# One instruction for the decay products, six bias rows folded away, scores in four 64x64 tiles, and new lists

## The reference, cut to what matters

```python
# one layer; l = 0 on ctx, l = 1 on x, l = 2 on both outputs
k = key @ kW.T + kb;  q = query @ kW.T + kb;  v = values @ vW.T + vb
sc = softmax(where(dam, q @ k.T / sqrt(32), NEG))      # first softmax
dist = sqrt((sum(sc) - cumsum(sc)) * |i - j|)
te = clip(exp(dist * -softplus(gammas)), 1e-5, 1e5)
att = softmax(where(mask & dam, scores * te, NEG)) @ v
x = layernorm(query + att @ oW.T + ob) * ln1_g + ln1_b
if l != 1:                                             # feed-forward
    x = layernorm(x + relu(x @ w1.T + b1) @ w2.T + b2) * ln2_g + ln2_b
# cross attention of x on ctx
scores = (x @ wq) heads (ctx @ wk).T / 4 * pad - (1 - pad) * 1e10
x = layernorm(softmax(scores) @ (ctx @ wv) @ wo + bo + x) * ln_gamma + ln_beta
```

## Time and profile before

| | value |
|---|---|
| median of 3 runs | 3373.02 us (3371.89 to 3376.1) |
| the profiled execution | 3372.7 us, its span 3371.0 us |
| PE busy | 2990.0 us, 89% |
| DVE busy | 2802.8 us, 83% |
| ACT busy | 2715.9 us, 81% |
| POOL busy | 775.8 us, 23% |
| mean granted TensorE clock | 0.97 |

### The profile page before, as it was taken

The page is one execution under the profiler, slowest core; times in us unless marked ns, Lnnn a source line. Parts: engine busy times, 40 slices in busy tenths (PEclk is TensorE's granted clock), DMA queues, the critical chain, the costliest instruction groups (busy, mean ns, idle before and its releaser), DMA issues.

```text
span 3371.0 us, 71476 instructions
## 1 busy us (share of the span) xinstructions
PE 2990.0 (89%) x19520; PEld 2204.6 (65%) x19520; DVE 2802.8 (83%) x5825; ACT 2715.9 (81%) x10244; POOL 775.8 (23%) x1111
## 2 busy tenths in 40 slices
PE   2689999999999999999999999999999998999986
PEld 1466676666676666676666666666666666666664
DVE  3688988888988888988888988888988888988883
ACT  1688888888888888888888888888888887888883
POOL 1212222222222222222222221222221222221221
PEclk9799999999999999999999999999999999999998
DMA  5000101000101000101100001000101101001100
GB/s 160 20 25 25 32 25 33 27 26 25 30 25 33 27 26 25 30 25 33 28 26 25 29 24 33 29 26 25 28 24 33 29 28 29 24 24 33 29 17 10
DMA packets 166407, 101.66 MB, mean 30 GB/s; under 512 B 36697, under 2 KB 165709, under 8 KB 166221
## 3 DMA queue, kind: packets, MB, share of 16 engines
q1 hardware_dynamic: 166220, 99.97, 10.4%
HBM read 56.26 MB, written 10.01 MB: 20 GB/s over the span
## 4 chain that ended last, share of the span: by engine, by line
PE 55%; DVE 19%; issue 12%; SPq 4%; ACT 3%; DMA 2%; POOL 1%; DVEq 0%; ACTq 0%; POOLq 0%
PE gen_ps L623 17%; PE gen_ps L755 13%; PE gen_ps L709 6%; PE gen_ps L673 4%; SPq L556 4%; PE gen_ps L690 3%; DVE E L920 3%; PE scores_ps L664 2%; ACT X L802 2%; PE scores_ps L652 2%; DVE X L929 2%; PE gen_ps L718 2%; PE gen_ps L631 2%; PE gen_ps L684 2%; DVE res L964 2%
## 5 line engine op out<-in xcount | busy, mean ns | idle before, releaser
L802 ACT ACTIVATE X<-X,nm 128x128 f32<-128x128 f32 x1536 | 596.0, 405 | 56.7 <-DVE nm L945 55.8
L802 ACT ACTIVATE E<-scores_ps,nm 128x128 f32<-128x128 f32 x1536 | 542.3, 406 | 24.2 <-DVE nm L912 24.0
L912 DVE TENSOR_REDUCE nm<-scores_ps 128x8 f32<-128x1024 f32 x320 | 390.3, 1220 | 182.0 <-PE scores_ps L652 113.6
L623 PE MATMUL gen_ps<-f_buf,up_w 128*128 128x256 f32 x2048 | 466.1, 383 | 0.8 <-ACT f_buf L459 0.8
L1052 POOL TENSOR_SCALAR_AFFINE_SELECT X<-X 128x1024 f32<-128x1024 f32 x192 | 211.2, 1100 | 1100.8 <-DVE X L939 1100.0
L755 PE MATMUL gen_ps<-down_w,hidden 128*128 128x256 f32 x2048 | 459.7, 379 | 0.0
L802 ACT ACTIVATE X<-scores_ps,nm 128x128 f32<-128x128 f32 x1024 | 362.3, 400 | 116.6 <-issue 60.9
L673 PE MATMUL gen_ps<-ident,X 128*128 128x128 f32 x2560 | 380.0, 283 | 79.2 <-ACT xv_t L476 39.8
L929 DVE SCALAR_TENSOR_TENSOR X<-E,rz,decay 128x128 f32<-128x128 f32 x1536 | 431.0, 350 | 3.7 <-DVE E L920 0.5
L920 DVE TENSOR_TENSOR_SCAN E<-chain,E 128x1024 f32<-128x1024 bf16 x192 | 429.8, 2238 | 0.0
L623 PEld LDWEIGHTS gen_ps<-f_buf,up_w 128*128 128x128 f32 x2048 | 382.7, 191 | 70.5 <-issue 21.9
(11 more groups left out here) (124 smaller groups left out, 5491.7 us busy)
## 6 DMA issues: line engine op xcount, KB each, us to landing
k_diag<-k_f SPq DMA_DIRECT2D x768, 32.0 KB, 1.9
xk_diag<-xk_f SPq DMA_DIRECT2D x1024, 8.0 KB, 1.8
ctx_f<-in_ctxT SPq DMA_DIRECT2D x32, 256.0 KB, 3.2
ctx_t<-in_ctx SPq DMA_DIRECT2D x32, 256.0 KB, 2.8
x_f<-in_xT SPq DMA_DIRECT2D x32, 256.0 KB, 2.6
x_t<-in_x SPq DMA_DIRECT2D x32, 256.0 KB, 2.6
cx_f<-in_ctxT SPq DMA_DIRECT2D x32, 256.0 KB, 2.7
out<-out_t SPq DMA_DIRECT2D x32, 256.0 KB, 2.2
```

The lines of the kernel that those rows point to most:

```text
L623: mm = nc.tensor.matmul(ps[:, i * T:(i + 1) * T], w[:, k, c * P:(c + 1) * P], src[:, k, :], start=(k == 0), stop=(k == C - 1))
L802: a = nc.scalar.activation(dst[:, cols], src[:, cols], ACT.Exp, bias=minus_max[:, h:h + 1], accum_out=sums[:, h:h + 1])
L912: nc.vector.tensor_reduce(nm1[:, UNIT[u], :], unit_heads(scores_ps[SLOT[u]][:, :]), AX_X, ALU.max, negate=True).then_inc(max1_done, 1)
```

## The change

It does five things.

1. `dist` loses its reciprocal, and `x` becomes one tensor_tensor of 1024 columns (scan times decay). The reciprocal of the sums moves behind the square root: a new POOL step `zroot` computes -(z1 ** -0.5) for eight columns in two instructions, and `effect` on ACT becomes eight activations of 128 columns whose scale is that column.
2. Of nine bias rows three stay (o of layers 0 and 1, v of layer 2). vb of layers 0 and 1 is folded into ob by matmuls with o_w, the other four (ob of layer 2, both b2, bo) are added to norm_b in the prologue, and what they would add behind a norm is taken out of up_bias, k_bias and a new q_bias. `q` on its reader becomes two instructions with a bias.
3. The mask (or padding) and the scores matmuls are each four 64x64 tiles. dam_bias has a new layout, filled by 24 DMAs rather than 3; pad_bias is loaded by two DMAs. The waits of `scores` stand apart from the matmuls.
4. The prologue gets 4 matmuls of 256 columns and 40 of one column on PE for the folds, with DVE work and three DMAs behind them, before the first projection. The three row_bias DMAs now wait for this.
5. All lists and BANKS are new. TENSOR and SYNC hold the same steps in another order. From SCALAR to VECTOR go up (0,2), (0,3), (2,1); k 0; q; turn (0,2), (2,1), (0,1); pt (3,1,0) both halves, (2,0) half 0, (0,1) both, (1,0) half 0. From VECTOR to SCALAR go v 1, v 2; up (2,0); pt (3,0,1) half 1, (3,0,0) both, (3,1,1) half 1. POOL gets six zroot steps.

```diff
 def distance(now, d, u):
-    for i in range(UH):
-        ins = nc.vector.scalar_tensor_tensor(out=X[:, p, i * S:(i + 1) * S],
-                                             in0=E[:, E_SLOT[u], i * S + 1:(i + 1) * S + 1],
-                                             scalar=rz1[:, UNIT[u], i:i + 1], in1=decay[:, l, i, :],
-                                             op0=ALU.mult, op1=ALU.mult)
-    ins.then_inc(x_done, 1)
+    nc.vector.tensor_tensor(X[:, X_SLOT[u], :], E[:, E_SLOT[u], 1:UW + 1],
+                            decay[:, u[0], :, :].rearrange("p h s -> p (h s)"), ALU.mult).then_inc(x_done, 1)
 def effect(now, d, u):
-    nc.scalar.activation(x, x, ACT.Exp, scale=-1.0).then_inc(te_done, 1)
+    act.wait_ge(zroot_done, zroot_order.upto(now, d, ("zroot", u)))
...
+    for i in range(UH):
+        cols = slice(i * S, (i + 1) * S)
+        a = nc.scalar.activation(x[:, cols], x[:, cols], ACT.Exp, scale=rz1[:, n, i:i + 1])
+    a.then_inc(te_done, 1)
+def zroot(now, d, u):
+    n = UNIT[u]
+    wait_apart(pool, exp1_done, exp1_order.upto(now, d, ("exp1", u)))
+    nc.gpsimd.tensor_tensor(rz1[:, n, :], z1[:, n, :], neg_half[:, :], ALU.pow).then_inc(zpow_done, 1)
+    wait_apart(pool, zpow_done, zroot_order.upto(now, d, ("zroot", u)))
+    nc.gpsimd.tensor_scalar(rz1[:, n, :], rz1[:, n, :], -1.0, None, ALU.mult).then_inc(zroot_done, 1)
 # scores
+for bank, half in quarters:                      # (0,0), (0,1), (1,0), (1,1)
+    rows = halves[bank]
+    dst = out[halves[half], bank * BANK:(bank + 1) * BANK]
+    if is_layer(u):
+        nc.tensor.matmul(dst, ident_bf[rows, rows], dam_bias[u[0]][rows, half, :], start=True, stop=False)
...
+for i in range(n):                               # n = 2 for a layer unit, 1 for a cross unit
+    for bank, half in quarters:
...
+        mm = nc.tensor.matmul(out[halves[half], bank * BANK + i * wide:bank * BANK + (i + 1) * wide],
+                              q[rows, i if is_layer(u) else u[2], queries], keys,
+                              start=False, stop=(i == n - 1))
 # prologue on PE
+for l in range(2):
+    for k in range(C):
+        mm = nc.tensor.matmul(rows_ps[0:ROWS, 0:D], v_cols[:, l, k, :], o_w[l][:, k, :], ...)
+def fold(col, w, which):
+    for k in range(C):
+        mm = nc.tensor.matmul(cols_ps[:, col:col + 1], w[:, k, :], bias_cols[:, which, k:k + 1], ...)
...                                              # 16 folds of up_w, 2 of k_w, 2 of xq_w
 # prologue on SP
-for l in range(L):
-    sp.dma_start(dam_bias[l][:, :, :], src).then_inc(toeplitz_in, 16)
+for l in range(L):
+    for bank in range(2):
+        for c in range(C):
+            for half in range(2):
+                sp.dma_start(dst.rearrange("p (j s) -> p j s", s=S), src).then_inc(toeplitz_in, 16)
...
+sp.wait_ge(rows_ready, 1)
+for i in range(3):
+    sp.dma_start(row_bias[i:i + 1, :, :], rows_parts[:, i, :]).then_inc(rows_out, 16)
```

Of the new orders the prediction speaks of these stretches:

```diff
 TENSOR
-(1, ("down", 2)), (0, ("att", (0, 1))), (0, ("att", (0, 0))), (1, ("turn", 2, 2))
+(1, ("down", 2)), (0, ("att", (0, 1))), (1, ("vx",)), (1, ("turn", 2, 2))
-(1, ("scores", (3, 0, 1))), (0, ("pt", (1, 1), 1)), (0, ("att", (1, 0))), (0, ("att", (1, 1))), (1, ("scores", (3, 0, 0)))
+(1, ("scores", (3, 0, 1))), (1, ("scores", (3, 0, 0)))
 VECTOR
-(1, ("sums", 2, 2)), (0, ("max2", (1, 0))), (0, ("scores2", (1, 1))), (1, ("tok", 2, 2))
+(1, ("sums", 2, 2)), (0, ("max2", (1, 0))), (1, ("tok", 2, 2))
 POOL
+(0, ("zroot", (1, 0))), (2, ("dev", 3, 1)), (0, ("zroot", (1, 1))), (0, ("widen", (0, 1))), (0, ("select", (1, 0)))
```

More of the change, by code:

```diff
@@ L34 @@
 FIRST_KEY_MASK = [1, 1, 0]
+BIAS_COLS = 6
+ROWS = 3
+O_ROWS, V2_ROW = (0, 1), 2
 FFN_LAYERS = [0, 2]
@@ new lines @@
+POOL = [(1, ("dev", 0, 2)), (1, ("widen", (2, 1))), (0, ("zroot", (0, 1))), (1, ("widen", (2, 0))),
+    (0, ("zroot", (0, 0))), (0, ("select", (0, 0))), (1, ("dev", 2, 1)), (0, ("select", (0, 1))),
+    (0, ("zroot", (1, 0))), (2, ("dev", 3, 1)), (0, ("zroot", (1, 1))), (0, ("widen", (0, 1))),
+    (0, ("select", (1, 0))), (0, ("widen", (0, 0))), (1, ("dev", 2, 2)), (0, ("select", (1, 1))),
+    (0, ("widen", (1, 0))), (0, ("widen", (1, 1))), (0, ("dev", 0, 1)), (0, ("dev", 1, 1)),
+    (1, ("widen", (3, 0, 1))), (1, ("widen", (3, 0, 0))), (1, ("widen", (3, 1, 0))), (0, ("zroot", (2, 1))),
+    (0, ("zroot", (2, 0))), (0, ("select", (2, 1))), (0, ("select", (2, 0))), (1, ("widen", (3, 1, 1)))]
@@ L191 @@
     kind_order(SCALAR, kind) for kind in ("ln", "root", "effect", "exp2", "spread"))
-select_order, dev_order, wide_order = (kind_order(POOL, kind) for kind in ("select", "dev", "widen"))
+select_order, dev_order, wide_order, zroot_order = (kind_order(POOL, kind) for kind in ("select", "dev", "widen", "zroot"))
 GEN_BANKS = 4
@@ L583, in load @@
                     wait_apart(sp, scores_done, scores_order.upto(now, d, last, 1))
-                    sp.dma_start(pad_bias[0:3, :], pad_parts_dram[:, tok]).then_inc(done, 16)
+                    for first in (0, HALF):
+                        sp.dma_start(pad_bias[first:first + 3, :], pad_parts_dram[:, tok]).then_inc(done, 16)
             def store(now, g, d):
@@ new lines, in scores @@
+                halves = [slice(i * HALF, (i + 1) * HALF) for i in range(2)]
+                quarters = ((0, 0), (0, 1), (1, 0), (1, 1))
+                wait_apart(pe, scores_free[p], bank_order[p].before(now, d, ("scores", u)))
+                if not is_layer(u):
+                    wait_apart(pe, loaded["pad_bias"], 32 * (g + 1))
+                for bank, half in quarters:
[3 more added lines that the diff above has]
+                        nc.tensor.matmul(dst, ident_bf[rows, rows], dam_bias[u[0]][rows, half, :], start=True, stop=False)
+                    else:
+                        bias = pad_bias[rows, b * S:(b + 1) * S].unsqueeze(1).to_broadcast([HALF, BANK // S, S])
+                        nc.tensor.matmul(dst, pad_ones[rows, :], bias, start=True, stop=False)
@@ L708, in out_proj @@
                     for c in range(C):
-                        nc.tensor.matmul(out, att[:, b, c, :], w[:, c, :], start=(c == 0), stop=False)
-                    mm = add_row(out, row)
+                        mm = nc.tensor.matmul(out, att[:, b, c, :], w[:, c, :], start=(c == 0), stop=(c == C - 1 and l > 1))
+                    if l < 2:
+                        mm = add_row(out, O_ROWS[l])
                 return mm
@@ L869, in _, with split @@
             link(nc.vector.tensor_scalar(pads[:, :], pads[:, :], -1.0, PAD_BIAS, ALU.add, ALU.mult))
-            for whole, parts in ((pads, pads_parts), (rows, rows_parts)):
+            def split(whole, parts, ready):
                 for i in range(3):
```

226 lines of the change are left out of this document (131 added, 95 removed), and 52 rows, old and new, of tables (SCALAR, TENSOR, VECTOR).

## The result

The changed kernel takes 3452.89 us (median of 4 runs, 3451.61 to 3454.56) against 3373.78 for the kernel before, measured beside it: 1.0234 times as long, interval 1.0217 to 1.0252. 3291 was predicted, with 3190 to 3395 as range: the time is slower and outside the range, 162 us above the forecast.

What follows compares the result with a forecast made beforehand. It took PE's work, 92.4 us of a 100.64 us turn, plus some 8 us of waiting as the bound. Prologue 86 + 31 turns of 97.2 + 190 ramp and run out + 1.7 gave 3291 us, range 3190 to 3395.

Steps and rivals of the forecast that it cites:

- Durations and work: Busy time a turn after the change: PE 88.2 us, ACT 88.5, DVE 85.3, built from traced instruction times.
- bound of 99 us a turn: Upper bound for the turn: PE waits 10.8 us, called midway to DVE's present 13.9.
- rival of weights that show between 64x64 tiles: PE's score tiles: 32 sets each show 0.10 us of weight loading, turn 100.5, total 3397 us; chance 0.06.
- What is taken from PE counts nearly whole, until ACT or DVE is as full: Work removed from PE, 92.4 to 88.2 us a turn, was to shorten the turn almost fully.
- A turn after ... 97.2: Turn after the change, down from 100.64 us, with waits of 9.0 on PE, 8.7 ACT, 11.9 DVE.
- from 7 to 21 us on 24.0, still the emptiest ... which hides it: POOL's six powers and negations add 7 to 21 us a turn, hidden by 5.3 us of other work.
- new orders answer for that: POOL's list: dev, widen and select wait behind the power's wait on exp1; reordering was to deal with it; no size.
- POOL late: POOL's widen and power meet scans, delaying select, dev and tok twice a turn by 1 us: 99.2, 3355 us; chance 0.07.
- ACT takes over: The effect on ACT, in every unit's chain, lengthens waits to 13 us: turn 101.5, total 3430 us; chance 0.13.
- Some 2 of the 3.4 us there should go: PE's longest gap, ahead of the transpose of x_tok, shrinks by some 2 us, perhaps with the slow clock stretch.
- what is late next I can't read: The next late step in the new lists was left unnamed; a slipped DVE tok could cost PE up to 5 us.
- The prologue: Before the first projection: mask DMAs, norm rows and folds add 26 to 37 us, taken as +29, to 86 us.

## Why the prediction was wrong

By its own steps:

- **Durations and work: right.** PE 89.2 against 88.2; the folds' rows 1.1 where 1.3 was forecast; the tiles 1.8 where 2.6 was forecast for the old lists (2.9 less the 0.3 of two cross units side by side), though each unit measures as worked out (0.24 and 0.96). ACT 88.1 against 88.5, effect 2.4 us as from the earlier trace rows; in the new lists part 1 adds 7.6 to ACT (88.0 less 80.4; 8.0 forecast, though the row it names gives 8.6) and takes 6.0 from DVE (6.5 forecast). The read-outs that move to DVE are 2.5 us (84.7 to 80.6 on ACT is the forecast 4.0, 87.0 to 89.5 on DVE is half of its 5.0). In the bound of 99 us a turn, midway from 8.2 to 13.9 is 11.1 and not 10.8; nothing hangs on it. The rival of weights that show between 64x64 tiles is refuted by 0.96 us from the scores to the next group, where four sets that showed 0.10 each would have given 1.36. The rule that the prediction quotes beside it from the Trainium skill (TensorE: Matmul & The Clock Gate) stands there in the section "The mechanism"; the trace disagrees with it, as the prediction says.
- **"What is taken from PE counts nearly whole, until ACT or DVE is as full": this step failed.** Taken from PE in the old lists, 3.5 us brought 1.0, 1.8 brought none, 1.1 brought 0.5. Folds and tiles alone have 99.9 a turn where the prediction's terms gave 96.7: 3.2 of the 5.2 us by which the turn was missed. The new lists added 2.5 and part 1 none, where the forecast had 0.5 for both together (96.7 to 97.2). The step was wrong already in the kernel before, where ACT and DVE had 16.1 and 13.9 us to spare. As I read it, the 8.2 us for which PE stood still were not a remainder that shrinks but places in the lists where PE waits for a result of DVE or ACT: the wait for x_tok kept its 115 us when PE had less to do.
- **"A turn after ... 97.2": the term that was mis-sized, by 5.2 us a turn.** The waits were put at 9.0 on PE by leaning on those of before. Measured are 13.2, of them 6.4 for `rz_wide`. Two of its causes have a price in these lists: 3.4 for the power and 1.7 for the effect's seven more instructions. That the two prices add was not run; if they do, the changed kernel without both would have 97.3, about the turn that was forecast, and the forecast had charged the turn with neither.
- **POOL: "from 7 to 21 us on 24.0, still the emptiest ... which hides it": wrong.** The added load was 42.1 - 26.0 = 16.1 us a turn, inside the bounds, but it is not hidden: without the power's computing the turn is 3.4 us shorter. The 5.3 us of other work were to hide it, and don't: 1.7 of the 3.4 us go when `effect` stops waiting for the power, so that wait was not hidden, and 1.7 stay all the same, with what stands behind the power in POOL's list. A power that meets the scan ends 1.46 us behind it, 3.5 in all; two of six do. And "new orders answer for that" was a hope: the new order puts the power ahead of widen (2, 0), where PE stands for 4.24 us in each turn, and for 2.49 without the power's computing.
- **The rivals.** "POOL late" had the engine, and its sign came: PE's gaps end on POOL. It had a turn of 99.2, 2 us over the forecast; the power's computing alone measures 3.4, and the delay fell on widen and not on select, dev and tok. Whether the meeting with the scan costs what the rival had it cost was not run. "ACT takes over" had its mechanism too, and 101.5. It was weighed at 0.13 with one of its own arguments against it ("ACT's present waits are mostly of an engine with time to spare"). The old lists show how far it holds: ACT at 92.4 us of work in a turn of 105.8 has 58% of the chain, although it stands idle for 13.4 us. In the changed kernel both rivals act at once, which no case allowed for; the two taken together (the turn forecast, 97.2, plus 4.3 and 2.0) would have given 103.5, above the 102.4 measured.
- **The other lists.** "Some 2 of the 3.4 us there should go" was right about the place (PE's wait for x_tok: 115.0 us in all before, 48.6 after) and wrong about the worth. The answer to "what is late next I can't read" is widen (2, 0), 4.24 us, with the slow clock behind it as before. The lists by themselves cost 4.1 us a turn for the old code, a cost for which the prediction has no term; PE's wait for `rz_wide`, 143.7 us in all where it was 14.4, is where it shows.
- **The prologue: right.** +26.5 against +29, 83.45 against 86 (82.4 to 85.9 in the nine kernels with this prologue). The tiles have 11.4 of it (forecast 11 to 13), the folds 12.8 (forecast 15 to 24). That part of it could be had back by moving twelve DMAs was not seen.

Left open: why 1.8 us of tiles bring nothing and 1.1 us of folds bring 0.5 in the same lists, what the meeting of power and scan costs, and why part 1, with its ACT load taken away again, is still 1.5 us a turn slower than the kernel before in the old lists. The tiles' case has one trace: DVE's waits for the scores are 164.9 us with them and 113.6 and 116.2 without (before, folds alone). None of the three is settled by a run.

## What to carry to other kernels

Where three engines in fixed orders are each busy for 81 to 92% of a turn, busy time does not price an edit: work taken away was worth 0 to 0.5 of itself here, and six powers a turn on the emptiest engine cost 3.4 us or nothing, by the lists around them. Price each new instruction by the moment at which its input is ready, what the other engines do at that moment, and what stands behind it in its own list. And a change that comes with new orders is two changes: run the old code with the new orders and the new code with the old ones before believing in either. And a turn is a mean over many: where turns alternate, the median is the length of one kind.
